# Layer 1's attention: probabilities normalised ahead of their transposes, V stationary, output leaving the array transposed

## What is computed

```
q, k, v = split_heads(x @ Wq), split_heads(x @ Wk), split_heads(x @ Wv)
sim  = einsum('bhid,bhjd->bhij', q, k) * scale
sim  = where(adjacency_mask[:, None], sim, -max)
attn = softmax(sim, axis=-1)
out  = einsum('bhij,bhjd->bhid', attn, v)
out  = out.transpose(0, 2, 1, 3).reshape(B, N, INNER) @ Wo + bo
```

## Time and profile before

| | |
|---|---|
| time, median of 3 runs | 1881.68 us (1880.18 to 1883.77) |
| the profiled execution's own time | 1882.32 us |
| its span, first to last instruction | 1880.5 us |
| mean granted TensorE clock | 0.988 of full speed |
| PE busy | 1821.2 us, 97% of the span |
| DVE busy | 1276.4 us, 68% |
| ACT busy | 886.5 us, 47% |
| POOL busy | 652.2 us, 35% |
| layer 1, its 32 groups | about 350 to 643 us |

### The profile page before, as it was taken

How to read it: one execution, slowest core, us unless ns; L and a number is a source line. 1 busy time by engine, 2 the same in 40 slices (tenths; PEclk the granted TensorE clock), 3 DMA queues, 4 the chain that set the end, 5 groups by cost and what they waited for, 6 DMA issues and landing times. The chain is left out here.

```text
span 1880.5 us, 75019 instructions
## 1 busy us (share of the span) xinstructions
PE 1821.2 (97%) x31280; PEld 1739.5 (93%) x31280; DVE 1276.4 (68%) x2919; ACT 886.5 (47%) x1997; POOL 652.2 (35%) x841
## 2 busy tenths in 40 slices
PE   7999999799999899999999999999999889999998
PEld 7899999799999799999999999999999889999997
DVE  6777777577767545555565555555555569999997
ACT  5777777455555523333333333333333335555554
POOL 3565665222222110000000000000000068999897
PEclk9999999899999999999999999999999999999999
DMA  3322322443323211011111011110111012222222
GB/s 108 88 74 85 85 75 79 123 138 91 97 85 101 90 30 37 24 33 32 34 34 29 28 29 34 34 34 23 32 31 34 19 47 78 68 68 78 76 68 64
DMA packets 149459, 113.65 MB, mean 60 GB/s; under 512 B 43008, under 2 KB 148864, under 8 KB 149376
## 3 DMA queue, kind: packets, MB, share of 16 engines
q1 hardware_dynamic: 149376, 112.46, 20.6%
HBM read 78.87 MB, written 33.55 MB: 60 GB/s over the span
## 5 line engine op out<-in xcount | busy, mean ns | idle before, releaser
L281 POOL TENSOR_TENSOR ln_rstd<-ln_var_eps,minus_half 128x2 f32<-128x2 f32 x128 | 91.3, 713 | 979.6 <-DVE ln_var_eps L274 976.9
L188 PE MATMUL banks<-ln_hT_hi,square_w_hi_held 128*128 128x256 f32 x512 | 152.4, 298 | 3.9 <-DVE square_w_lo_held L675 3.2
L299 ACT ACTIVATE ln_h<-ln_x,ln_shift,ln_rstd 128x256 f32<-128x256 f32 x256 | 140.0, 601 | 25.0 <-DVE ln_shift L288 18.7
L188 PE MATMUL banks<-ln_hT_hi,l_g_w_hi 128*128 128x256 f32 x512 | 148.6, 290 | 2.5 <-PEq L2081 2.5
L1782 ACT ACTIVATE l_cat_hi<-banks 128x512 fp32r<-128x512 f32 x128 | 66.3, 603 | 172.7 <-PE banks L1986 172.7
L188 PE MATMUL banks<-l_wh_w_hi,ln_hT_hi 128*128 128x256 f32 (+1 forms) x512 | 145.2, 284 | 0.0
L188 PE MATMUL banks<-l_cat_hi,l_aw_hi 128*128 128x256 f32 x512 | 145.1, 283 | 0.0
L189 PE MATMUL banks<-ln_hT_lo,square_w_hi_held 128*128 128x256 f32 x512 | 143.6, 281 | 0.0
L190 PE MATMUL banks<-ln_hT_hi,square_w_lo_held 128*128 128x256 f32 x512 | 143.4, 280 | 0.0
L190 PE MATMUL banks<-ln_hT_hi,l_g_w_lo 128*128 128x256 f32 x512 | 142.5, 278 | 0.0
L190 PE MATMUL banks<-l_wh_w_hi,ln_hT_lo 128*128 128x256 f32 (+1 forms) x512 | 142.5, 278 | 0.0
(11 more groups left out here) (231 smaller groups left out, 6392.2 us busy)
## 6 DMA issues: line engine op xcount, KB each, us to landing
hidden<-y SPq DMA_DIRECT2D x96, 256.0 KB, 2.1
ln_x<-hidden SPq DMA_DIRECT2D x96, 256.0 KB, 2.7
x_res<-hidden SPq DMA_DIRECT2D x96, 256.0 KB, 2.9
ln_x<-x SPq DMA_DIRECT2D x32, 256.0 KB, 2.8
x_res<-x SPq DMA_DIRECT2D x32, 256.0 KB, 3.0
out<-y SPq DMA_DIRECT2D x32, 256.0 KB, 2.1
l_adj_u<-adj SPq DMA_DIRECT2D x96, 16.0 KB, 2.3
l_stage_attn<-L_attn SPq DMA_DIRECT2D x4, 256.0 KB, 3.2
```

Source lines behind the costliest of these rows:

```text
L188: nc.tensor.matmul(out, lhs(lh), rhs(rh), start=start, stop=False, skip_group_check=True)
L281: self.nc.gpsimd.tensor_tensor(self.rstd[:, g.slot], self.var_eps[:, g.slot], self.core.minus_half[:, 0:PAIRS], ALU.pow).then_inc(self.rst ...
L299: last = self.nc.scalar.activation(self.h[:, u, p, :], self.x[:, u, p, :], ACT.Relu, bias=self.shift[:, u, p:p + 1], scale=self.rstd[:, u, ...
```

## The change

It takes the branch `direct` away from the arithmetic of attention and keeps a flag `small_heads` (true in layer 0) for the parts that depend on the number of tiles. In layer 1:

- VectorE sums the probabilities (L721's instruction, 128x512) and takes the reciprocal, between the variance and the shift of the layer norm; GpSimd multiplies the probabilities by it, between its root and its mask; the reciprocal from PSUM and the two scalings at the end of VectorE's step go, and so does the column of ones in V with its memset.
- TensorE transposes the weighted probabilities later: not between keys and output projection, but after the first half of `values` (6 matmuls); the second half (6) follows them.
- PV holds V as the stationary operand and moves the transposed probabilities (64 columns for 65), writing the output already transposed to banks 6 and 7. `transpose_o` (four 128x128 transposes and its wait) goes. The evacuation of the output reads banks 6 and 7 in place of bank 0; its size is unchanged.
- Layer 0 keeps its instructions; some waits outside the loop are added that were not issued before.

```diff
-    direct = heads == 8
-    VW = HD if direct else HD + 1
+    small_heads = NT == 2
...
-        v = sb("v", [P, 2, PAIRS, 2, HPC, VW], F32, HELD if direct else MOVED)
+        v = sb("v", [P, 2, PAIRS, 2, HPC, HD], F32, HELD)
...
-        probT = sb("probT", [P, 2, NT, BLOCKS, P], F32, MOVED if direct else HELD)
+        probT = sb("probT", [P, 2, NT, BLOCKS, P], F32, MOVED)
...
+        z = sb("z", [P, 2, NT, ROWS_OF_TILE])
+        weighted = sb("weighted", [P, 2, NT, ROWS_OF_TILE, S])
+        if small_heads:
             oT = sb("oT", [P, 2, KC, TOK])
-        else:
-            o = sb("o", [P, 2, PAIRS, D])
...
-        B_OT = 6 if direct else 0
+        B_OT = 6
...
-            if not direct:
-                nc.gpsimd.memset(v[:, :, :, :, :, HD:VW], 1.0).then_inc(made.sem, 1)
...
                 if gn is not None:
                     ln.root(pool, gn)
-                if direct and c2.exists(groups):
+                if c2.exists(groups):
                     for t in range(NT):
                         after(pool, rz_ready, c2, t + 1)
                         known(pool, probT_in_psum, c2.back(2), t + 1)
...
-                        last = nc.scalar.activation(oT_hi[:, e.slot], ps[:, B_OT, :].rearrange("p (c t) -> p c t", c=KC),
-                                                    ACT.Copy)
+                        last = nc.scalar.activation(oT_hi[:, e.slot], ps[:, B_OT:B_OT + KC, 0:TOK], ACT.Copy)
...
                     if gn is not None:
                         ln.statistics(dve, gn, first=False)
+                    if c2.exists(groups):
+                        weights_of_rows(0)
+                    if gn is not None:
                         ln.shifts(dve, gn)
...
-                if not direct and c2.exists(groups):
-
-                    bank = ps[:, B_O:B_O + KC, 0:PAIRS * HPC * VW].rearrange("q c (p h e) -> q p c h e", p=PAIRS, e=VW)
-                    after(dve, o_in_psum, c2)
-                    nc.vector.reciprocal(rz[:, c2.slot, 0].rearrange("q (p c h) -> q p c h", p=PAIRS, c=KC),
-                                         bank[:, :, :, :, HD]).then_inc(rz_ready.sem, 1)
-                    after(dve, rz_ready, c2)
-                    known(dve, oT_in_psum, c2.back(2))
-                    r_of = rz[:, c2.slot, 0].rearrange("q (p c h) -> q p c h", p=PAIRS, c=KC)
-                    for c in range(KC):
-                        last = nc.vector.tensor_tensor(
-                            o[:, c2.slot, :, c * P:(c + 1) * P].rearrange("q p (h e) -> q p h e", e=HD),
-                            bank[:, :, c, :, 0:HD], r_of[:, :, c].unsqueeze(3).to_broadcast([P, PAIRS, HPC, HD]), ALU.mult)
-                    last.then_inc(o_ready.sem, 1)
...
-                def transpose_o():
-                    after(pe, o_ready, e)
-                    known(pe, ln.hT_lo_ready, e.back(-2))
-                    for c in range(KC):
-                        for p in range(PAIRS):
-                            last = nc.tensor.transpose(ps[:, B_OT, c * TOK + p * P:c * TOK + (p + 1) * P],
-                                                       o[:, e.slot, p, c * P:(c + 1) * P], core.ident)
-                    last.then_inc(oT_in_psum.sem, 1)
-
...
-                def transpose_prob(src, ready, t):
-                    after(pe, ready, c2, t + 1)
+                def transpose_prob(t):
+                    after(pe, weighted_ready, c2, t + 1)
                     if NT == 1:
                         known(pe, probT_ready, c2.back(1), 1)
-                    pr = src[:, c2.slot, t].rearrange("p h t -> p (h t)")
+                    pr = weighted[:, c2.slot, t].rearrange("p h t -> p (h t)")
...
-                if not direct and e.exists(groups):
-                    transpose_o()
...
-                if not direct and c2.exists(groups):
-                    transpose_prob(prob, prob_ready, 0)
                 if e.exists(groups):
                     project_out()
...
-                    values()
-                if direct and c2.exists(groups):
-                    transpose_prob(weighted, weighted_ready, 0)
+                    values((0, 1) if small_heads else (0,))
+                if c2.exists(groups):
+                    transpose_prob(0)
+                if not small_heads and b1.exists(groups):
+                    values((1,))
                 if gn is not None:
...
-                                            ps[b * S:(b + 1) * S, B_O + c, col:col + VW],
-                                            probT[r, u, 0, hp * PAIRS + p, b * S:(b + 1) * S],
-                                            v[r, u, p, b, hp], start=True, stop=True, skip_group_check=True)
-                        last.then_inc(o_in_psum.sem, 1)
...
+                                            ps[hp * HD:(hp + 1) * HD, B_OT + c, col:col + S], v[r, u, p, b, hp],
+                                            probT[r, u, t, (hp - 2 * t) * PAIRS + p, b * S:(b + 1) * S],
+                                            start=True, stop=True, skip_group_check=True)
+                    last.then_inc(oT_in_psum.sem, 1)
```

More of the change, by code:

```diff
@@ L540, in step @@
                     after_dma(pool, adj_loaded, g, apart=core)
-                    (known if direct else after)(pool, scores_in_psum, g.back(2), apart=core)
+                    known(pool, scores_in_psum, g.back(2), apart=core)
                     if static_mask is None:
@@ L561, in step @@
                                             ALU.add).then_inc(x_bo_ready.sem, 1)
-            run_steps(pool, step, groups, 3 if direct else 2)
+            run_steps(pool, step, groups, 3 if small_heads else 2)
         @block.scalar
@@ L614, in exponential @@
                     after(act, shifted_ready, c2, t + 1)
[L615 removed]
+                    known(act, weighted_ready, c2.back(2), t + 1)
                     nc.scalar.activation(prob[:, c2.slot, t], shifted[:, c2.slot, t], ACT.Exp,
@@ L620, in evacuate_v @@
                     after(act, v_in_psum, b1)
-                    known(act, oT_in_psum if direct else o_in_psum, b1.back(2))
+                    known(act, oT_in_psum, b1.back(2))
                     for c in range(KC):
@@ L632, in evacuate_T @@
                     return last
-                if not direct and c2.exists(groups):
+                if not small_heads and c2.exists(groups):
                     exponential(0)
@@ L694, in _ @@
             dve.wait_ge(core.constants_ready.sem, 1)
-            if not direct:
-                dve.wait_ge(made.sem, 1)
             def step(g):
@@ L763, in step @@
                     after(dve, v_in_psum, b1)
-                    known(dve, oT_in_psum if direct else o_in_psum, b1.back(2))
+                    known(dve, oT_in_psum, b1.back(2))
                     for c in range(KC):
@@ L792, in _ @@
                 for _ in range(WARM):
-                    nc.tensor.matmul(ps[:, B_O, 0:P], core.ident, core.ident, start=True, stop=True)
+                    nc.tensor.matmul(ps[:, B_OT, 0:P], core.ident, core.ident, start=True, stop=True)
                 ln.transpose(pe, g0, B_HT)
@@ L817, in project_T, with project @@
                 return last
-            def project(n, src_hi, src_lo, bank):
+            def project(n, src_hi, src_lo, bank, pairs=range(PAIRS)):
                 split_of(n)
-                for p in range(PAIRS):
+                for p in pairs:
                     for c in range(KC):
@@ L957, in step @@
                     known(pe, v_dve_ready, c2, apart=core)
-                    if not direct:
-                        after(pe, probT_ready, c2, apart=core)
-                        known(pe, o_ready, c2.back(1), apart=core)
+                    known(pe, oT_hi_ready, c2.back(1), apart=core)
+                    known(pe, oT_lo_ready, c2.back(1), apart=core)
+                    for t in range(NT):
+                        after(pe, probT_ready, c2, t + 1, apart=core)
                         for p in range(PAIRS):
-                            for hp in range(HPC):
-                                col = (p * HPC + hp) * VW
-                                for b in range(2):
+                            for b in range(2):
+                                col = (2 * p + b) * S
+                                for hp in range(HPC) if NT == 1 else (2 * t, 2 * t + 1):
                                     for c in range(KC):
```

84 lines of the change are left out of this document (29 added, 55 removed).

## The result

The changed kernel takes 1873.7 us, median of 5 runs (1870.75 to 1874.63), against 1881.95 (1880.18 to 1883.77) of the kernel before in the same session: a ratio of 0.9949, interval 0.9936 to 0.9961. The forecast was 1874.0. The profiled execution took 1874.63 us with a span of 1872.8 and a granted clock of 0.989; its counterpart of before 1882.32, 1880.5 and 0.988.

The account below looks back on a forecast made before the run. TensorE's instruction list bounds layer 1 before, the chain through VectorE and GpSimd after. Savings of 7.2 - 0.8 + 0.5 + 1.4 = 8.3 us give a median of 1873.4, forecast as 1874.0 us; range 1867.5 to 1882.0.

Parts of the forecast that it names:

- TensorE's list: Layer 1's loop: TensorE's instructions bound the kernel before; removing `transpose_o` takes 0.44 us a step from them.
- The chain: Layer 1, mask through VectorE's maximum, sum, reciprocal and GpSimd's product to the probabilities' transposes: 6.05 us, the new bound.
- TensorE's readiness: Layer 1's loop: TensorE ready for the probabilities' transposes 5.85 us after the mask, so it waits 0.20 us.
- B: Rival for layer 1's loop: the chain is hidden, TensorE bounds the step at 8.20 us; 1868.0 us total, chance 0.13.
- the branch: Layer 1's loop: 0.12 us a step for the branch in every second step and the layer's odd step, kept unchanged.
- A: The forecast itself: the chain through VectorE and GpSimd bounds layer 1's step at 8.40 us; chance 0.52.
- The step: Layer 1, mask to mask: 6.05 + 1.19 + 1.16 = 8.40 us, 8.52 with the branch against 8.76; 7.2 us in thirty steps.
- Covers: Layer 1: layer norm's application could slip 1 us; half of `values` helps hide ScalarE's evacuation, which uncovered costs 0.6 us.
- The ends: Layer 1's ends: step 2 loses 0.8 us, steps 32 and 33 save 0.5, the last stretch gains 1.4.
- The sum: Whole kernel: 7.2 - 0.8 + 0.5 + 1.4 = 8.3 us saved, all in layer 1.
- C: Rival: GpSimd's product in layer 1 takes 1.30 us, each step 0.26 longer; 1881.8 us, no change; chance 0.15.
- E: Rival: TensorE's sequencer loses its lead, adding "issue" pauses ahead of PV and scores, 0.49 us a step; 1888.7, chance 0.12.

Follow-up runs that it names:

- e4: Changed kernel with four 128x128 transposes of the identity added on TensorE between queries and keys of layer 1: 1884.92 us, ratio 1.0011.
- e6: Kernel before with one of its four output transposes kept, so layer 1's output is not the reference's: 1875.37 us, ratio 0.9953.
- e1: Changed kernel with the next group's statistics moved from the middle of VectorE's chain to behind `y`, one step earlier: 1872.1 us, ratio 0.9932.
- e2: Changed kernel with `split_oT` put ahead of the statistics on VectorE, nothing else changed: 1882.66 us, ratio 0.9999.
- e3: Changed kernel with GpSimd's product done twice in layer 1, first into scratch space: 1906.03 us, ratio 1.0127.
- e10: Changed kernel with six extra reciprocals into scratch space on VectorE, between the reciprocal of the sums and the shift: 1873.11 us, ratio 0.9957.
- e5: Changed kernel with all 12 matmuls of `values` ahead of the probabilities' transposes, instead of six on either side: 1882.77 us, ratio 1.0021.
- e8: Changed kernel run again without edit, in another session beside e9 on the same chip: 1875.43 us, ratio 0.9966.
- e9: Kernel of e1 run again without edit, on the same chip as e8: 1867.91 us, ratio 0.9923.

## Why the prediction was right, point by point

**TensorE's list.** `transpose_o` was put at 0.44; e4 measures 0.44. That the list was the bound before is shown by e6.

**The chain.** Forecast from the mask: maximum 1.03, sum 3.95, product 4.95 to 5.99, transposes 6.05. Measured: 1.10, 4.03, 5.03 to 6.07, 6.13. Two links were short: scores to maximum by 0.07 (layer 0's rows stood in for layer 1's; e1 and e2 have 1.10 too), and maximum to `ln_var_eps` by 0.02 (2.86 for 2.84). The four links from sum to transposes were right to 0.01 (0.72, 0.28, 1.04, 0.06). e2 and e3 show that a step follows this chain one for one.

**TensorE's readiness.** Forecast 5.85, so a wait of 0.20. e1, in which the chain doesn't bind, has 5.94, and 6.13 less 5.94 is 0.19. The size is right, but the sum put all of it at the transposes and nothing at the output projection, whose wait for `split_oT` it named only for step 33. In the loop the wait at the transposes is 0.09 to 0.14, and the rest is lost at the projection (e1). It makes no difference to the time, since the transposes come when the chain lets them. Both sides came late by the same 0.08 to 0.09, TensorE because part of its projection matmuls stood 0.118 apart and not 0.113. The step forecast here for B (8.20, and 8.32 with the branch) is about what e1 reaches: 8.24 for the shorter step, 8.33 and 8.34 on average. B was a matter of 0.2 us, as the text had it, and fell for the reason given for A.

**The step.** From the transposes to the mask 1.19 and 1.16 were forecast; the row above has 1.19 (551.48 to 552.67) and 1.16 (552.67 to 553.83). The shorter step is 8.48 against 8.40: the chain is 0.08 longer, and this is the mis-sized term. The 0.12 that was kept for the branch held two things. In the kernel before, short and long steps alternate at 8.64 and 8.81, which is 0.09 on average; the rest was mostly step 32 with its 9.47. After, they alternate at 8.48 and 8.62, 0.07 on average. So an ordinary step gained 0.18 (8.73 to 8.55) where 0.24 was forecast, 1.8 us less in thirty steps.

**Covers.** The shift lasts 0.16 as forecast; that the application can slip by 1 us without cost is shown by e10, which moved it by 0.99. The evacuation of the probabilities behind half of `values` is a cover that e5 takes away in part (the rows' transposes stay as cover). It costs 0.41 ahead of PV and 0.20 a step; the text's 0.6 was the evacuation's full length.

**The ends.** Step 2 came to 8.01 (forecast 8.0). In steps 32 and 33 the shift lasts 0.16 for 1.23, as argued, and 0.5 had been put for both. Step 32 alone gained 0.98, 0.80 more than an ordinary step. Behind the last mask 1.30 us were saved, where 1.4 and step 33's part of the 0.5 had been put. Together that is 2.1 for a forecast 1.9. In step 33 PV now waits 0.34 us for ScalarE's evacuation of the probabilities, which the forecast hadn't named, because no second half of `values` is left there to cover it:

```profile
630.85 0.69 PE L933 MATMUL banks<-l_probT,l_v 64*64 64x64 f32 x32 [0.34 <-ACT l_probT L643]
```

**The sum.** Layer 1 gave 6.7 for a forecast 8.3: 1.8 too much in the ordinary steps, 0.2 too little at the end. The medians differ by 8.25, and that this meets the forecast within 0.3 us is luck: in another session the changed kernel stood 6.2 us under the kernel before (e8). The difference between 6.7 and 8.25 lies outside layer 1, where times spread by more than that, as shown below.

**The other rivals.** C: the product took 1.04 us in layer 1, not 1.30. E: a sequencer without its lead would show more "issue" ahead of PV and the scores; the waits have 5.0 and 6.0 us in thirty steps, 0.17 and 0.20 each, as in the earlier trace rows, and the longer of the alternating steps exceeds the shorter by 0.14, where it was 0.17. Neither happened. One small difference shows elsewhere: from the transposes to the next matmul it is 0.41 where they have waited for the product (changed kernel, e2, e3) and 0.35 where they haven't (e1, e4). That is the 0.04 seen in e1. The kernel before has 0.41 there too without such a wait, so what makes the difference isn't shown.

## What to carry to other kernels

When work leaves the engine that bounds a loop, add up the chain that would bind next, link by link from rows, and compare it with the time at which the relieved engine would be ready: here both lay within 0.2 us, and on one chip the place of the statistics in VectorE's order decided between no gain (e2), 6 us (e8) and 11 to 14 us (e1 and e9). Look at what stands inside that chain without belonging to it; the statistics of the next group cost 0.2 us a step there and nothing that showed behind `y`. Look too for instructions in the chain that something else waits for: `split_oT`, on its way, held the output projection up by 0.1. And a filler between an instruction and the one that reads its result is worth its place: moved away, it left 0.24 us of bare latency.

## What the runs showed of the hardware that was not expected

**Two paces of the same matmuls.** The projections' matmuls of 128x256 stand 0.1133 us apart in the whole loop of the kernel before, and 0.1133 or 0.1178 apart, by stretches that repeat from step to step, in the changed kernel and in e1, e2, e4 and e6, at a granted clock of 1.00 in the loop's window of the changed kernel as of the kernel before. e6 has the old layout and e4 the transposes between queries and keys, e1 no wait; so none of these three alone is the cause. The cause is open, and the slower pace is worth about 0.09 us a step at the transposes.

**Statistics to aggregation.** Back to back, the two statistics instructions and what reads them are 0.89 us apart from start to start, against 0.66 to an instruction that doesn't read them, with 0.15 idle in the row (e2).

**Layers that weren't touched.** Layer 1 repeats to 0.06 us from one execution of the changed kernel to another, but it began 3.9 us later in the second. Windows of the changed kernel:

```profile
357.59:639.58 281.99, 275.30 (x3965) 251.84 (x3965) 196.31 (x481) 170.31 (x329) 105.97 (x127) 1.00 0.36 105
```

and of e8:

```profile
361.52:643.57 282.05, 275.32 (x3965) 250.49 (x3965) 196.38 (x481) 170.28 (x329) 105.89 (x127) 1.00 0.35 103
```

What comes behind layer 1, from the next layer's first matmul to the end, is the same code in all twelve kernels, and it took 1231.8 us (e10) to 1237.5 (e1), with 1234.8 in the kernel before and 1233.2 in the changed one. That is why a single total of this kernel is worth less than the windows of the layer in question.
